# Six matmuls of the v projection placed one by one between the head pairs of P times V

## The reference

```python
qkv = x @ Wqkv                    # 128 -> 3 * 1024; x has half of its channels shifted by one token
q, k, v = jnp.split(qkv, 3, -1)
q = l2norm(q) * qs;  k = l2norm(k) * ksc
q = q * cos * scale + rotate_half(q) * sin * scale
k = k * cos / scale + rotate_half(k) * sin / scale
sim = jnp.einsum('bhwie,bhwje->bhwij', bq, bk2) * QK_SCALE    # bk2: own window and the one before
attn = jax.nn.softmax(jnp.where(mask, -jnp.finfo(sim.dtype).max, sim), -1)   # P
out = jnp.einsum('bhwij,bhwje->bhwie', attn, bv2)             # P times V
x = out.transpose(0, 2, 1, 3).reshape(b, n, INNER) @ Wo + x
x = ffn_layer(shift_tokens(x), ...) + x
```

## Time and profile before

| | us |
|---|---|
| median of 3 runs | 3832.99 |
| lowest and highest | 3829.45, 3838.61 |
| the profiled execution's own time | 3835.11 |
| its span, first to last instruction | 3833.3 |
| TensorE busy in the span | 3290.7 (86%) |
| VectorE, ScalarE, GpSimd busy | 2808.5, 2595.7, 2500.6 |

### The profile page before, as it was taken

One profiled execution on the slowest core, in us unless ns is written; L12 is line 12 of the kernel. 1 busy time (PEld: TensorE's weight loads), 2 busy tenths in 40 slices (PEclk: granted clock), 3 DMA queues, 4 the chain that ended last, 5 costly groups with the idle time before them and its releaser, 6 DMA issues.

```text
span 3833.3 us, 127009 instructions
## 1 busy us (share of the span) xinstructions
PE 3290.7 (86%) x52864; PEld 2810.5 (73%) x53056; DVE 2808.5 (73%) x4272; ACT 2595.7 (68%) x3787; POOL 2500.6 (65%) x2289
## 2 busy tenths in 40 slices
PE   3444448999989999899999899999999998999996
PEld 2333236888878888788888788888787887888885
DVE  5766766777777777777777777777777777777772
ACT  2222225777777777777777777777777776777774
POOL 1000007777777877777777777778777777787771
PEclk7666668999999999999999999999999999999997
DMA  1000001111111111111111111111111111111111
GB/s 56 0 0 0 0 0 35 50 41 35 35 29 40 56 34 35 35 41 41 47 35 35 34 37 59 35 35 35 35 37 55 35 35 31 41 37 30 36 34 31
DMA packets 54643, 130.05 MB, mean 34 GB/s; under 512 B 10944, under 2 KB 28864, under 8 KB 53312
## 3 DMA queue, kind: packets, MB, share of 16 engines
q1 hardware_dynamic: 54080, 122.02, 10.9%
HBM read 19.25 MB, written 2.10 MB: 6 GB/s over the span
## 4 chain that ended last, share of the span: by engine, by line
PE 72%; ACT 12%; DVE 7%; issue 7%; POOL 1%; DMA 0%; SPq 0%; ACTq 0%; DVEq 0%; POOLq 0%
PE pair L217 58%; PE pair L220 14%; ACT qT L737 7%; ACT sq L727 2%; DVE qT L362 1%; ACT ss L732 0%; DVE VA L347 0%; DVE qT L353 0%; DVE wq_l L843 0%; ACT qT L275 0%; DVE tab L835 0%; ACT qT L272 0%; DVE VB L358 0%; DVE qT L326 0%; DVE qT L316 0%
## 5 line engine op out<-in xcount | busy, mean ns | idle before, releaser
L966 POOL TENSOR_TENSOR qk<-qk,ts 128x1024 f32<-128x1024 f32 x384 | 914.8, 2383 | 312.2 <-DVE ts L857 293.4
L945 POOL TENSOR_TENSOR qk<-qk,rn 128x1024 f32<-128x1024 f32 x384 | 729.3, 1921 | 43.1 <-issue 28.3
L853 DVE TENSOR_TENSOR qk<-pair,tab 128x1024 f32<-128x1024 f32 x384 | 468.6, 1220 | 373.0 <-ACT sq L719 370.3
L217 PE MATMUL pair<-wq_h,xs_h 128*128 128x512 f32 x1152 | 515.2, 447 | 34.7 <-issue 15.0
L220 PE MATMUL pair<-small,qk 128*128 128x128 f32 x3192 | 452.5, 285 | 66.7 <-ACT qT L737 49.4
L714 ACT ACTIVATE Sx<-Sx 128x1024 f32<-128x1024 f32 x192 | 203.7, 1061 | 413.9 <-DVE Sx L870 413.9
L220 PEld LDWEIGHTS pair<-small,qk 128*128 128x128 f32 x3192 | 361.0, 146 | 151.3 <-issue 127.5
L857 DVE TENSOR_TENSOR ts<-pair,tab 128x1024 f32<-128x1024 f32 x384 | 466.5, 1215 | 0.0
L217 PE MATMUL pair<-wq_h,xs_l 128*128 128x512 f32 x1152 | 464.8, 403 | 0.0
L861 DVE TENSOR_REDUCE ss<-sq 128x16 f32<-128x1024 f32 x384 | 464.3, 1209 | 0.0
L217 PE MATMUL pair<-wq_l,xs_h 128*128 128x512 f32 x1152 | 460.8, 400 | 0.0
(11 more groups left out here) (204 smaller groups left out, 6959.1 us busy)
## 6 DMA issues: line engine op xcount, KB each, us to landing
VB<-VA SPq DMA_DIRECT2D x192, 384.0 KB, 3.5
VB<-VA SPq DMA_DIRECT2D x96, 128.0 KB, 3.4
wq_raw<-wqkv SPq DMA_DIRECT2D x6, 1536.0 KB, 8.8
xf<-xT SPq DMA_DIRECT2D x96, 64.0 KB, 1.9
xf<-xT SPq DMA_DIRECT2D x96, 63.8 KB, 2.0
wo_sb<-wo SPq DMA_DIRECT2D x6, 512.0 KB, 3.6
out<-X SPq DMA_DIRECT2D x8, 256.0 KB, 2.3
w_raw<-fw SPq DMA_DIRECT2D x6, 341.0 KB, 8.0
```

The source lines that it names most:

```text
L217: return T_.matmul(out, lhsT, rhs, start=start, stop=stop, **k)
L853: V_.tensor_tensor(h3(qk[:, now, kind, :], DH), h3(source[:, :], DH), rep(tab[:, 2 * kind, b, :], HEADS, DH), ALU.mult)
L945: G_.tensor_tensor(x, x, bc(rn[:, then, kind * HEADS:(kind + 1) * HEADS], HEADS, DH), ALU.mult).then_inc(S["scaled"], 1)
L966: G_.tensor_tensor(qk[:, now, kind, :], qk[:, now, kind, :], ts[:, kind, :], ALU.add).then_inc(S["added"], 1)
```

## The change

A function `project_part` issues one of the six matmuls of a projection. In `step_pe`, within the loop over head pairs of P times V, matmul j of v follows head pair a = j + 1, for j from 0 to 5; so two head pairs come ahead of the first, and one between each two that follow, and the last head pair comes after all six. The waits for `rotated` and, in the first step of a turn, for the low part of v's weights stand ahead of the first of them, and `v_done` is signalled by the last. The old place of the v projection is kept for the steps that have no P times V, which are the first three. The number of instructions with work in them is the same. ScalarE's, VectorE's, GpSimd's and SyncE's lists are not changed.

```diff
+        def project_part(pair, high, low, first, j):
+            u = j // 3
+            cols = slice(first + u * UNIT, first + (u + 1) * UNIT)
+            return mm(pair[:, u * UNIT:(u + 1) * UNIT], (high, low, high)[j % 3], (wq_h, wq_h, wq_l)[j % 3][:, cols],
+                      j % 3 == 0, j % 3 == 2)
...
                                 last = mm(PB[odd * DH:(odd + 1) * DH, to:to + WIN],
                                           values[rows, ring, head * DH:(head + 1) * DH], PT[rows, a, q0:q0 + WIN])
+                    j = a - 1
+                    if pl.has(0) and 0 <= j < 6:
+                        if j == 0:
+                            e.wait_ge(S["rotated"], blocks(pl, "rotated", 0, 1))
+                            if fresh:
+                                e.wait_ge(S["wq_low_v"], layers(pl, 1, t // NBLOCKS, 1))
+                        vlast = project_part(one, high, low, 2 * INNER, j)
+                        if j == 5:
+                            vlast.then_inc(S["v_done"], 1)
                 last.then_inc(S["av_done"], 1)
...
-            if pl.has(0):
+            if pl.has(0) and not pl.has(3):
                 e.wait_ge(S["rotated"], blocks(pl, "rotated", 0, 1))
```

## The result

| | before | after |
|---|---|---|
| median, us (4 runs each, same chip) | 3834.48 | 4249.10 |
| lowest and highest | 3829.45, 3838.61 | 4247.85, 4255.12 |
| profiled execution: time, span | 3835.11, 3833.3 | 4255.12, 4253.3 |

The changed kernel is slower: the ratio is 1.110, with a 95% interval of 1.107 to 1.112 (the two medians give 1.108). That is +415 us, where +438 was forecast (4271 us).

What follows compares the result with a forecast made beforehand. TensorE's own list plus its waits was taken as the bound. 94 odd steps at 2.91 (273.5), 94 even at 1.27 (119.4), 91 at 0.6 (54.6) and -10 for issue gave +438 us: 4271 us, range 4035 to 4410.

Steps and rivals of the forecast that it cites:

- Part 1: In P times V, each of v's six matmuls put alone forces tile-size changes costing 0.30 us, range 0.15 to 0.36.
- Its four pieces: Per v matmul: 0.145 into wide tiles, 0.09 slow first wide one, 0.09 going back, 0.01 longer first row.
- The upper of the two sums: Price of tile-size changes per v matmul: 0.335 us, or 0.245 if the slow first wide matmul isn't met.
- the signs: Expected in the changed profile: 0.16 us from small matmul to v's next, then 0.33 to 0.41 to small ones.
- Rival (a): Single tile-size changes in P times V cost next to nothing, 0 to 0.15 us; at 0, 3934 us; chance 0.10.
- (c): Tile-size changes in P times V cost more, at 0.5 us each: +675, 4500 us; chance 0.08.
- Rival (b): Instruction handout bounds P times V, so TensorE gets ahead during v: 3650 us hidden wholly, about 3790 half; chance 0.04.
- Part 2: After k's transposes, v no longer covers ScalarE's kT copy: with tile-size changes, odd steps +2.91 us, even steps +1.27 us.
- The bare wait: In odd steps the transposes of `xf` wait uncovered for ScalarE's kT copy, some 1.45 us, 94 times.
- Part 3: In even steps ScalarE's later list delays the gelus and VectorE's maximum: 0.6 us, bounds 0 to 0.8.
- Part 4: TensorE's 59.6 us of pauses marked "issue", mostly in P times V, stay or shrink: -10 us, from -30 to +15.
- Rival (d): The clock falls as TensorE's work gets gaps: 7.5 us in each of 94 pairs, +700 on top; chance 0.04.

## Why the prediction was right

**Its reading of the bound** held: TensorE's own list sets the time, and 110.05 of 114 us are busy after too.

**Part 1** forecast 0.30 us per matmul of v alone and was measured at 0.33, and 0.32 per place by the three runs with one, three and six places. Its four pieces, read from rows about quite other neighbours, came out as 0.11 (0.145), 0.10 (0.09), 0.085 (0.09) and 0.02 (0.01). The upper of the two sums, 0.335, was the right one; taking 0.30 was a hedge without a reason. Of the signs, the wide matmul starts 0.13 after the last small record, for 0.16, and the small ones 0.43 after it, for 0.33 to 0.41. The product lasts 2218.47 - 2213.33 + 0.10 = 5.24 us to its last record, against 5.08. The Trainium skill, "TensorEngine Tiling (Array Packing)", Key Properties, has the direction (a change of tiling mode drains the engine), and the runs agree that each change costs time. The estimate of 0.31 us from "TensorE: Matmul & The Clock Gate" in the Trainium skill, Single matmul latency, was as near as the hedge, though that formula is given for a bf16 matmul on the full array and for no change of tile size.

Rival (a), free switches, is out by the runs with one, three and six places, and so is (c), 0.5 us and more. Rival (b), that TensorE gets ahead in its list while v streams, is out as well: no row of small matmuls runs quicker than 0.117 behind any insertion.

**Part 2.** In odd steps `xf` starts 2238.98 - 2231.31 = 7.67 us after the product's start, for 7.51 forecast and 4.60 before: +3.07 for +2.91. In even steps the feed-forward matmuls start at 6.22, for 6.06: +1.43 for +1.27. Both misses are six times the 0.03 of part 1. From the transposes of k to those of `xf` it is 2.29 us, for 1.10 + 1.03 + 0.14 = 2.27 forecast. The bare wait was put at 1.45 us and is worth 1.39 by the edit that takes it away; the profile shows 1.21. The third group of six needed no wait to speak of (1.8 us in all, at L217 for kT). That the wait for `rotated` doesn't bind was right as well; with v ahead of the product it does, 57 us.

**Part 3** was mis-sized: 0.6 forecast, 0.32 measured. Gelu starts 9.76 us after the product's start (9.73), and the record of the gating ends at 11.52 (11.50). But the maximum could not have started at 10.88: TensorE's feed-forward matmuls came 0.16 later than forecast, which puts it to 11.04, and it did start at 11.44, 0.08 ahead of the end of the gating's record. So it is late by 0.40 and not by 0.62, and 0.32 of it comes through; where the last 0.08 goes is not shown. The term was the difference of two chains, and part 1's price moved only one of them: kT's copy too started 0.16 later than forecast (6.50 for 6.34), but the copy of v followed it after 0.92 us instead of 1.05. The mechanism is shown by the edit to ScalarE's list: 0.32 us a pair gone, 29 us, of which 19 are seen in the time.

**Part 4** was mis-sized too: -10 forecast, with -30 as its bound, and -39 us measured (59.6 to 20.5). The step that failed is "50 x (1.2 - 0.3), and a part of it stays": of the pauses in the product nothing stays (44.4 us by the label), and the four at the boundaries of turns, which the sum counted among the 50, grow by 5.5. By the starts the product lost 58.5 us before; a part of that cost nothing, since a step with a pause had no wait for qT.

The sum with the measured terms is 94 x 3.07 + 94 x 1.43 + 91 x 0.32 - 39 = 413 us, against 420 between the two spans. The forecast's 438 came about with parts 1 and 2 too low by 30 and parts 3 and 4 too high by 25 and 29: some of its accuracy is luck.

**What it said of the profile** was wrong in one sentence: that TensorE's busy time would hardly rise and its idle time by 200 us or more. It is the other way, +388 and +32: the price of a switch shows inside the records and not between them (the wide record of 0.50 us over a distance of 0.43).

Rival (d), a falling clock, did not come in the changed kernel (0.99 in both over the layers). But with the same places and narrower matmuls it came, behind a product without idle time, and not after gaps, as the rival had it. The chance of 0.04 was given for the wrong mechanism.

## What to carry to other kernels

Count places, not matmuls: on TensorE one round trip from small 64x64 tiles to these 128x128 matmuls and back cost 0.32 us whether one or six wide matmuls stood inside, and no row of waits shows it, so work that is to break up a long run of small tiles goes in as one block. Before work is moved, look for what it covered where it stood, and move something else there: v as one block, `xf` behind the feed-forward work and ScalarE's copies in the order in which they come ready turned 1.110 into 0.987. And where a term is the difference of two chains, an error in either goes into it whole: 0.16 us on TensorE's side took a quarter of the 0.6.

## What the runs showed of the hardware

**Pauses marked "issue" follow a block of instructions.** The DMA view of the kernel before about the pause of the earlier trace rows, which ends at 2026.11 (40 slices of 0.2 us; GB/s moved in each, then the queue of instructions with packets and MB):

```profile
GB/s 0 0 0 0 0 0 0 0 0 0 0 0 0 0 0 0 0 82 0 0 0 0 0 0 0 0 0 0 0 0 0 0 0 0 0 0 0 82 0 0
...
q8 instruction: 2, 0.03, 1.9%
```

The stretch is 2020 to 2028, so one packet of 0.2 x 82 = 16.4 KB moves at 2023.4, early in the product, and the pause ends 2.6 us later. Of the 49 long products of the kernel before, 48 have a gap, and every one of these has such a packet 2.2 to 2.9 us ahead of the gap's end; the 418 packets of the whole run would put one there by chance in under a tenth of cases each. With v behind it is all 41. The pauses come late in the product, mostly 100 or more of its 128 records in. And they come back at the same place of the loop's body: in the products that start at 1199.84, 1729.34, 2257.85, 2790.02 and 3325.16 us, 32 products apart, the pause follows record 123. The changed kernel has 106112 records of matmuls and weight loads and the same 418 packets, 254 records for each, so the queue is by all appearance TensorE's own. In the changed kernel such packets fall in the product too, and nothing waits; 2212 to 2228, slices of 0.4 us, with the products of the timeline above at 2213.3 to 2218.5:

```profile
GB/s 0 0 0 41 0 0 0 0 0 0 0 0 0 0 41 0 0 0 0 0 0 0 0 0 0 0 0 113 276 215 297 82 41 0 0 0 0 0 0 0
...
q8 instruction: 3, 0.05, 1.4%
```

By the length of the product from first row to last, and what stands in it: 1.77 us, 49 pauses; 2.72 with narrow matmuls between two pieces of eight rows, 27; 3.5 with a last piece of fourteen rows, 21; 3.5 with two of eight, one; 5.14 with six places, one. (With six places and narrow matmuls it is 4.10, and some thirty are longer; there it is the last rows that are stretched, all alike, at a granted clock of 0.88 over 904.1 to 908.6 us, so this is the clock and not a pause.) So it isn't the length of a piece alone. All of this fits one reading: a dense run of small matmuls uses up its instructions before the next block is there, and wide ones in its middle give it time. It is an inference; no run changed the size of a block or where the product lies in one. The Trainium skill, "Runtime: NRT & Kernel Launch", Instruction fetch mechanics, has blocks of 16 KiB, which agrees with the packets, and a cost of crossing from one to the next that is mostly hidden. That holds for most of the 418 before, but not for those that meet this product late: 48 pauses of some 1.1 us.

**The clock can fall with TensorE busy.** 0.93 over the layers, and 0.66 in a stretch with 4.93 of 5.00 us busy, with six narrow insertions a product; 0.99 over the layers with the same six together.

**Narrow matmuls don't scale with their columns.** With 128x128 weights and `float32r` operands, matmuls of 512 columns start 0.235 us apart, those of 256 columns in the feed-forward work 0.12 (2219.76, 2219.87, 2219.99 in the changed kernel), and those of 128 columns 0.11: half the columns halve the distance, and a quarter gains nothing more.
